# Hi and lo rows transposed by DMA instead of by TensorE in a graph network and expert kernel

## The reference, cut to what matters

```python
h = layernorm(x)
for l in range(3):
    h_neigh = segment_sum(h[src], dst) / deg
    rst = relu(h @ W_self[l] + h_neigh @ W_neigh[l] + b[l])
    h = rst / max(norm(rst), 1e-12)
x = x + h
xn = layer_norm(layernorm(x), ln_g, ln_b)
top2 of softmax(xn @ Wg), gelu(xn @ W1 + b1) @ W2 + b2 of those two, weighted and summed
x = x + layer_norm(layernorm(x) + combined, out_g, out_b)
```

## Time and profile before

| | us |
|---|---|
| median of 3 runs | 2334.58 (2333.9 to 2334.83) |
| the profiled execution | 2329.04 |
| its span, first to last instruction | 2327.3 |

### The profile page before, as it was taken

One profiled execution on the slowest core, in us unless ns is written; L12 is line 12 of the kernel. 1 busy time (PEld: TensorE's weight loads), 2 busy tenths in 40 slices (PEclk: granted clock), 3 DMA queues, 4 the chain that ended last, 5 costly groups with the idle time before them and its releaser, 6 DMA issues.

```text
span 2327.3 us, 45193 instructions
## 1 busy us (share of the span) xinstructions
PE 2108.8 (91%) x15947; PEld 1163.2 (50%) x15947; DVE 1784.6 (77%) x4201; ACT 990.4 (43%) x1698; POOL 1253.7 (54%) x1396
## 2 busy tenths in 40 slices
PE   1988889888799999999799999998389999999997
PEld 0444344334344444444344444444167777777775
DVE  4778887556587878887688787876479999999974
ACT  1222111111233333333333333332677777777761
POOL 3770003871455555554344444443658888888754
PEclk9999999999899999999899999999589999999998
DMA  4453335783355555554566666664546565565533
GB/s 129 138 153 120 109 118 132 116 114 107 121 170 163 168 167 170 163 168 144 167 206 209 211 210 205 209 212 165 158 108 143 129 138 136 129 138 135 132 49 43
DMA packets 162789, 343.48 MB, mean 148 GB/s; under 512 B 32153, under 2 KB 32327, under 8 KB 162567
## 3 DMA queue, kind: packets, MB, share of 16 engines
q0 software_dynamic: 60816, 165.43, 27.3%
q1 hardware_dynamic: 101751, 175.16, 25.5%
HBM read 175.81 MB, written 165.31 MB: 147 GB/s over the span
## 4 chain that ended last, share of the span: by engine, by line
PE 52%; DVE 18%; POOL 11%; issue 11%; ACT 6%; DMA 1%; DVEq 0%; POOLq 0%; ACTq 0%
PE psS L486 19%; PE psY L486 12%; PE psY L1696 9%; POOL node_info L633 4%; POOL slot_table L633 4%; DVE YB L1206 3%; DVE R L1322 3%; DVE HT L1199 3%; ACT HH L876 2%; POOL scl L728 2%; PE psT L1613 2%; DVE HH L1346 2%; PE psS L1720 1%; PE psT L1668 1%; PE psA L1653 1%
## 5 line engine op out<-in xcount | busy, mean ns | idle before, releaser
L486 PE MATMUL psY<-w_n,HT 128*128 128x512 f16 x2844 | 672.2, 387 | 82.8 <-DVE HT L1199 79.9
L486 PE MATMUL psS<-w_s,HT 128*128 128x512 f16 x2844 | 652.5, 379 | 0.0
L486 PEld LDWEIGHTS psY<-w_n,HT 128*128 128x128 f16 x2844 | 265.8, 99 | 474.7 <-DVE HT L1199 175.9
L486 PEld LDWEIGHTS psS<-w_s,HT 128*128 128x128 f16 x2844 | 268.6, 98 | 280.2
L868 ACT ACTIVATE RR<-R 128x512 f32<-128x512 f32 x237 | 149.4, 630 | 294.6 <-DVE R L1322 294.6
L735 POOL DMA_INDIRECT y_rows<-YB,poutT x158 | 161.0, 1019 | 187.9 <-DVE YB L1206 159.7
L728 POOL TENSOR_TENSOR scl<-ssm,halfpow 128x1 f32<-128x1 f32 x158 | 88.8, 562 | 286.5 <-DVE ssm L1340 286.5
L486 PE MATMUL psS<-w_w,raw 128*128 128x512 f16 x948 | 217.5, 379 | 0.0
L832 ACT ACTIVATE HH<-R 128x512 f16<-128x512 f32 x79 | 49.6, 628 | 373.1 <-DVE R L1187 373.0
L1216 DVE SCALAR_TENSOR_TENSOR SB<-psS,downs,bias 128x512 f32<-128x512 f32 x237 | 177.8, 750 | 12.1 <-PE psS L486 9.5
L1346 DVE SCALAR_TENSOR_TENSOR HH<-RR,scl,HH 128x512 f16<-128x512 f32 x158 | 118.7, 751 | 89.0 <-ACT HH L876 89.0
(11 more groups left out here) (280 smaller groups left out, 3680.5 us busy)
## 6 DMA issues: line engine op xcount, KB each, us to landing
self_rows<-SB SPq DMA_DIRECT2D x236, 256.0 KB, 2.0
Sl<-self_rows SPq DMA_DIRECT2D x158, 256.0 KB, 3.5
X<-in_x_dram SPq DMA_DIRECT2D x78, 256.0 KB, 2.8
y_rows<-YB SPq DMA_DIRECT2D x78, 256.0 KB, 2.2
out_dram<-obb SPq DMA_DIRECT2D x78, 256.0 KB, 4.2
raw<-in_L_gnn_W_neigh_dram SPq DMA_DIRECT2D x12, 256.0 KB, 4.5
raw<-in_L_gnn_W_self_dram SPq DMA_DIRECT2D x12, 256.0 KB, 4.8
y_rows<-YB,poutT POOLq DMA_INDIRECT x158, 3.0
```

The source lines that it names most:

```text
L486: mm = eng.matmul(acc, lhs[:, a, c, :], w[:, bpart, c, :], start=(n == 0), stop=(stop and n == 3 * KC - 1))
```

## The change

The transposes of HH are no longer matmuls. In every stage the sync engine issues one transposing DMA a tile (256 KB, SBUF to SBUF) from HH into HT, or into a slot of HTR. TensorE's `turn` and `turn_x`, VectorE's copy and ScalarE's copy `txc` are gone. The semaphores of a landed transpose are one per buffer, and HH is free again when the DMA has landed. In the sync engine's list `turn` has offset 1 and stands ahead of the stores, whose offset becomes -1 instead of 0; in stages 0 and 2 other functions stand in the list with it.

```diff
@@ sync engine
+            def turn(t, s):
+
+                i = t.slot(2)
+                sp.wait_ge(s.hhi, (t + 1).n)
+                sp.wait_ge(s.hlo, (t + 1).n)
+                after(sp, s.sp, (t + -1).n)
+                sp.dma_start_transpose(HT[i].rearrange("p a c n -> p (a c) n"), HH[i].rearrange("p a n -> p (a n)")
+                                       ).then_inc(s.ht[i], 16)
+
-            run_plan(TN, [(4, load_x), (0, store)],
+            run_plan(TN, [(4, load_x), (1, lambda t: turn(t, ph[0])), (-1, store)],
...
-                    run_tiles(T, [(0, store_self)])
+                    run_tiles(T, [(1, lambda t, s=s: turn(t, s)), (-1, store_self)])
...
-                    run_tiles(T, [(0, store_self), (5, load_self), (2, out_bias)], 1)
+                    run_tiles(T, [(1, lambda t, s=s: turn(t, s)), (-1, store_self), (5, load_self), (2, out_bias)], 1)
...
-            run_tiles(T, [(6, load_self3)], 2)
+            def turn_x(t):
+                t = t.own
+                i, q = t.slot(2), t.slot(FFN_RING)
+                sp.wait_ge(f3.xhi, (t + 1).n)
+                sp.wait_ge(f3.xlo, (t + 1).n)
+                after(sp, f3.down, (t + (1 - FFN_RING)).n)
+                sp.dma_start_transpose(HTR[q].rearrange("p a c n -> p (a c) n"), HH[i].rearrange("p a n -> p (a n)")
+                                       ).then_inc(f3.ht[q], 16)
+
+            run_tiles(T, [(6, load_self3), (-1, turn_x)], 2)
@@ ScalarE: hi0, hhi, and xhi alike
-                after(act, s.tr, (t + -1).n)
+                if t.t >= 2:
+                    act.wait_ge(s.ht[i], (t + -2).landed(2))
@@ VectorE
-            def turn(t, l):
-                s = ph[l]
-                i = t.slot(2)
-                dve.wait_ge(s.tr, (t + 1).n)
-                after(dve, s.sp, (t + -1).n)
-                dve.tensor_copy(HT[i][:, :, :, :], psT[i][:, :, :, :]).then_inc(s.ht, 1)
@@ TensorE
-                for a in range(2):
-                    for c in range(KC):
-                        mm = pe.transpose(psT[i][:, a, c, :], HH[i][:, a, c * P:(c + 1) * P], iden16[:, :])
-                mm.then_inc(s.tr, 1)
...
-                pe.wait_ge(s.ht, (t + 1).n)
+                pe.wait_ge(s.ht[i], t.landed(2))
...
-            run_tiles(T, [(4, lambda t: aggregate(t, 3)), (-2, turn_x), (-9, down), (4, carry_rest), (-7, turn_w),
+            run_tiles(T, [(4, lambda t: aggregate(t, 3)), (-9, down), (4, carry_rest), (-7, turn_w),
```

More of the change, by code:

```diff
@@ L142, in __init__ @@
         self.hlo = sem("p0_hlo")
-        self.tr = sem("p0_turned")
-        self.ht = sem("p0_ht")
+        self.ht = [sem(f"p0_ht{i}") for i in range(2)]
         self.y = sem("p0_y")
@@ L173, in __init__ @@
         self.hlo = sem("hlo")
-        self.tr = sem("turned")
-        self.ht = sem("ht")
+        self.ht = [sem(f"ht{i}") for i in range(2)]
         self.y = sem("y")
@@ L198, in __init__ @@
         self.xlo = sem("f3_xlo")
-        self.tx = sem("f3_tx")
-        self.txc = sem("f3_txc")
+        self.ht = [sem(f"f3_ht{i}") for i in range(FFN_RING)]
         self.gate = sem("f3_gate")
@@ L473, in build @@
         st6b = sb("st6b", [P, 6])
-        psX = psT[0]
         psWT = psT[1].rearrange("p a c n -> p (a c n)")
@@ L916, in xhi @@
                 act.wait_ge(f3.xn, (t + 1).n)
-                after(act, f3.tx, (t + -1).n)
+                if t.t >= 2:
+                    act.wait_ge(f3.ht[(t + -2).slot(FFN_RING)], (t + -2).landed(FFN_RING))
                 act.activation(HH[i][:, 0, :], XN[i], ACT.Copy).then_inc(f3.xhi, 1)
[L920 to L924, removed]
             def gate_tanh(t):
@@ L955, in fhi @@
                 act.activation(FH[i][:, 0, :], HS[i], ACT.Copy).then_inc(f3.fhi, 1)
-            run_tiles(T, [(4, lambda t: carry_hi(t, 3)), (-2, txc), (-8, fhi), (4, lambda t: relu(t, 3)),
+            run_tiles(T, [(4, lambda t: carry_hi(t, 3)), (-8, fhi), (4, lambda t: relu(t, 3)),
                           (4, sum_squares3), (4, carry_rest_in), (-7, weights_in), (-1, xn), (-1, xhi),
@@ L1276, in _ @@
             run_plan(TN,
-                     [(2, norm0), (0, lambda t: ylo(t, 0)), (1, lambda t: turn(t, 0)), (3, stats0),
+                     [(2, norm0), (0, lambda t: ylo(t, 0)), (3, stats0),
                       (0, lambda t: sev(t, 0))],
@@ L1350, in _ @@
                 run_tiles(T, [(5, lambda t, l=l: one_hot(t, l)), (2, lambda t, l=l: hlo(t, l)), (0, lambda t, l=l: ylo(t, l)),
-                                      (1, lambda t, l=l: turn(t, l)), (3, lambda t, l=l: carry_lo(t, l)),
+                                      (3, lambda t, l=l: carry_lo(t, l)),
                                       (3, lambda t, l=l: combine(t, l)), (3, lambda t, l=l: sum_squares(t, l)),
@@ L1627, in own @@
                 products(pe, psS[i][:, :], HT[i], WT[f"s{l}"]).then_inc(s.sp, 1)
-            run_plan(TN, [(0, lambda t: neigh(t, 0)), (1, lambda t: turn(t, 0)), (0, lambda t: own(t, 0))],
+            run_plan(TN, [(0, lambda t: neigh(t, 0)), (0, lambda t: own(t, 0))],
                      [(WSTEP(m) + 1, square_sums, m) for m in range(N_FIRST, len(NAMES))]
@@ L1656, in _ @@
             for l in (1, 2):
-                run_tiles(T, [(0, lambda t, l=l: neigh(t, l)), (1, lambda t, l=l: turn(t, l)),
+                run_tiles(T, [(0, lambda t, l=l: neigh(t, l)),
                                      (0, lambda t, l=l: own(t, l)), (3, lambda t, l=l: aggregate(t, l))], l - 1)
[L1660 to L1669, removed]
             def gate(t):
                 t = t.own
-                pe.wait_ge(f3.txc, (t + 1).n)
+                pe.wait_ge(f3.ht[t.slot(FFN_RING)], t.landed(FFN_RING))
                 after(pe, f3.logit, t.t)
```

## The result

The changed kernel takes 2472.98 us (median of 4 runs, 2450.52 to 2487.12) against 2334.7 (2333.9 to 2335.96): the ratio is 1.059, 95% interval 1.0556 to 1.0623. It is 138 us slower, where 47 less were forecast. The changed kernel also scatters more: 1.5% between its runs, against 0.1% before.

What follows compares the result with a forecast made beforehand. TensorE was taken as 98% busy in layers 1 and 2 and 99.9% in the last stage, layer 0 as mixed; -10 -55 +52 -33 = -46 from 2327.3 gave 2281, plus 7.3 made 2288 us; 8-in-10 range 2195 to 2900.

Steps and rivals of the forecast that it cites:

- the likeliest case: Whole kernel: transposes land in 3 to 5.2 us in layer 1, giving 2210 to 2330 us; chance 0.43.
- rival (B): SyncE's order and slower landings, 5.5 to 8 us in layer 1, without the DMA engines filling up: 2475 us; chance 0.24.
- What is removed: Transposes and copy wait: 0.66 us a tile less in layers 1 and 2; last stage 33 us less.
- Pieces and engine time: A transposed tile is 1024 runs of 256 bytes, 64 per engine: 2.4 or 6.0 us of engine time.
- The far end: Each transposing DMA, if written in pieces of 32 bytes, 8192 of them, takes 19.5 us of engine time.
- L alone: L, time from a transposing DMA's issue until the waiting matmul can start: 2.0 to 7.3 us, 4.5 taken in layers 0 and 1.
- The loop of layer 2: Transposing DMA waits behind load_self, which waits for combine; tile period P is 4.35 us plus half the landing time.
- the period of layer 2: Landing taken as 5.2 us, with 0.7 for transfers ahead, gives 6.95 us a tile against 6.29: 52 us more.
- Stage 0: Layer 0: quiet steps cost 3 us, scatter steps change nothing, VectorE's relief in 29 others gives 13: together 10 us less.
- Layer 1: Tile period P = 2.65 us plus half the landing time binds only from 5.9; at 4.5, TensorE's 5.62: 55 us less.
- Rival (C): DMA engines become the bound, from 2.4 to 2.9 us of engine time a transpose: 2643 at 4 us, 3275 at 6.0; chance 0.28.
- The signs of being wrong: Landing beyond 5.5 us, transpose issue taking microseconds, plain transfers landing much later, or a lower granted clock where TensorE waits.

Runs made afterwards that it cites:

- order2: Changed kernel with load_self at offset 4 instead of 5 in layer 2's sync-engine list; 2290.95 us, ratio 0.9828 to the kernel before.
- bias_early: Changed kernel with layer 2's bias store issued right behind the transposing DMA instead of ahead of the next one; 2325.1 us, ratio 0.9946 to the kernel before.
- order0: Changed kernel with load_x behind turn and store in stage 0's sync-engine list, same offset; 2408.76 us, ratio 1.0294 to the kernel before.
- nosl1: Changed kernel without 77 of layer 1's 79 gathers of the own rows (stale rows used); 2442.52 us, ratio 1.0462 to the kernel before.
- order02: Changed kernel with load_x behind turn and store in stage 0 and load_self at offset 4 in layer 2; 2216.13 us, ratio 0.949 to the kernel before.
- half2: Changed kernel with layer 2 transposing only the hi half (128 KB) by DMA; 2375.44 us, ratio 1.0187 to the kernel before.

## Why the prediction was wrong, point by point

It forecast 2288 us; the time was 2473, within the stated range of 2195 to 2900 but outside the likeliest case, and on the other side of no change. It is the time of rival (B), 2475, and in the main it has (B)'s cause, the sync engine's order and a slower landing. That the number fits to 2 us is luck: (B) took landings of 7 and 8 us in layers 1 and 2, and they were about 5.7 and 5.85. Nor is the DMA share under the 0.8 that was named for (B): it is 0.81 in layer 2 and 0.93 in layer 1.

In the profiles the forecast was 46 us less and the measured difference 121.5 more. Of the 167 us between them 87 lie in layer 2, 44 in stage 0, 30 in layer 1 and 6 in the last stage.

- **What is removed: right.** Where the landing is hidden, a tile takes 5.61 us (order2), as the 5.62 of products said, and the last stage is 27 us shorter where 33 were expected.
- **Pieces and engine time: right in size.** 1056 packets a tile were met, against 1024 assumed. Between 1200 and 1600 the changed kernel's queue has

```profile
q1 hardware_dynamic: 73024, 51.63, 56.0%
```

  that is 3584 us of engine time. The prediction priced a plain transfer at 128 packets; by the earlier trace rows it is 30114 / 210 = 143, and 144 in the packet records (128 of 2048 bytes, 16 of 4). So the window holds 73024 / (1056 + 3 x 144) = 49.1 tiles of 73.0 us. Less three plain transfers of 0.83 x 16 = 13.3 us each it is 33 us a tile, 2.1 us on each of 16 engines, 31 ns a piece. By the same count it is 1.5 us in bias_early and in order2. The prediction had 2.4 from the small packets. The far end, 19.5 us, is excluded. This goes against the Trainium skill (Advanced Engine Details and Errata, X-Bar Transpose), which has a transposing DMA as fast as a plain one: 1.5 to 2.1 us of engine time stand against 0.83 for a copy of as many bytes.
- **L alone: not far off.** The first transpose of the program, issued at 52.07 with little beside it, is waited for until 55.51: 3.4 us, of which 1.34 are the issue. The other page of the Trainium skill that was weighed (VectorE: DVE Perf Modes, the three transpose paths) has 1309 ns for one block; since eight land in 3.4 us, they don't follow one another.
- **The loop of layer 2: right in form, but not complete.** P = 4.35 + L/2 came from the earlier trace rows, and the changed kernel has its links: 3.54 us from `own` to the issue against 3.5. order2 takes that part away, and 177 us of layer 2 go. Two things were put at nothing: that `neigh` can be held up by the other loop behind a landed transpose, and that the products get slower behind long waits.
- **The step that failed: the period of layer 2, 2P = 2.6 + 0.9 + L + 5.19 with L = 5.2.** I gave 0.7 us for "two 256 KB transfers lie ahead on the same queue", read from how the bias lands behind the load in the earlier trace rows. The bias store directly ahead alone costs 2.0 us of landing (5.85 against 3.85 with that store behind). The 4.5 us that I took for a transpose without them was too long in turn (3.85 with the load ahead), so the two errors hide one another in part, and the landing was 5.85 where 5.2 stood. The larger part lies in what the formula left out: 1.08 us behind the landing, and 5.79 us of products instead of 5.19, at a granted clock of 0.92. Halved and times 79 the landing is 26 us, the time behind it 43, the products 24, the rest 2. 52 + 26 + 43 + 24 + 2 = 147, against the 139 measured. With the bias store behind the transpose all three are small (3.85, 0.28, 5.22), and 147 us of layer 2 go (bias_early). That a transposing DMA lands 2 us later behind a store was in no row, and I took a plain transfer's behaviour for it.
- **Stage 0: the sign was wrong.** 10 us less were forecast, 34 more came. The step took P = 3.55 + L/2 only for 14 quiet steps, said that nothing changes under GpSimd's scatters, and let VectorE's relief decide in 29 others. Under the scatters, from 370 to 530 us, 21 tiles pass instead of 24, which is some 20 of the 34 us (one ScalarE operation of each tile, line 856 in the changed kernel; before, then changed):

```profile
370.00:530.00 160.00, 13.78 (x24) 0.99 0.75 120
370.00:530.00 160.00, 12.52 (x21) 0.92 0.83 141
```

  The mean landing there is 6.2 us where 4.5 were taken, and it is waited for twice, by `neigh` and by `hhi` on ScalarE, which needs HH back (in all, times, longest us):

```profile
ACT HH L847 <- DMA HT<-HH: 38.6, 7, 7.2
PE psY L482 <- DMA HT<-HH: 34.9, 15, 5.8
```

  `load_x` ahead of the transpose costs as well: order0 takes 59 us from the stage by order alone.
- **Layer 1: half.** 55 us less expected, 25 came. L was taken as 4.5 us; its mean is about 5.7 (not all updates of layer 1 are in the trace), still under the 5.9 from which P = 2.65 + L/2 binds, but it passed that in some tiles (16 waits, 23.0 us). A mean under the threshold didn't keep single tiles under it. In nosl1, with one of GpSimd's gathers gone, one such wait is left.
- **Rival (C)** named room of 2.4 to 2.9 us of engine time as its point of decision. At 1.5 to 2.1 us it stayed below, and order2 shows layer 2 at a share of 0.97 with hardly a wait. **Rival (B)** was argued from four transfers that "already lie on the queue" of layer 2; the earlier trace rows show three a tile, and the transpose is the fourth.
- **The signs of being wrong.** Two of them came: an issue that takes 1.24 us or more where a plain one takes 0.32 to 0.46, and a lower granted clock. L passed 5.5 us by little (median 5.6 in layer 2, 5.2 in layer 1).

## What to carry to other kernels

A transfer that replaces work on an engine is only as good as its place in the issuing queue: before moving a step to a queue, list what each function ahead of it waits for, and put those whose wait comes late behind it, or give them an offset of one step less. Here that alone turned 5.9% slower into 5.1% faster (order02), and the bias store moved behind the transpose made it 5.5%. Where a period follows from a loop, P = (fixed + L)/2, the unknown latency should be sized with what lies directly ahead on its own queue, a store to HBM above all, and not from the landing of plain transfers. Such a formula is a lower bound: with two loops in turns on one engine, one holds the other up, and an engine that waits long may come back at a lower clock. Here these two cost more than the error in the latency.

## What the runs showed of the hardware that was not expected

- A transposing DMA of 256 KB occupies the sync engine's queue for 1.24 us or more (median 1.24 in stage 0 and layer 1, 1.47 in layer 2 of the changed kernel), against 0.32 to 0.46 for most plain ones. Half the size saves little: 1.29 in layer 2 of half2.
- Directly behind a 256 KB store to HBM its landing is about 2 us later than without (5.85 against 3.77 and 3.85 us); directly behind a second 256 KB load it is 0.8 us later (4.61).
- The DMA engines were kept at a share of 0.97 (266 to 281 GB/s) while layer 2 ran at 5.61 to 5.71 us a tile, nearly TensorE's own pace, with the transposes issued early.
- The busy time of the DMA engines for the same transfers isn't constant: 6.6 us a tile in layer 2 of the changed kernel, 5.5 in order2.
- Behind some waits TensorE's products start at the lower of the two clock levels: twelve take 4.28 us after a wait of 3.42 (at 1418.35) and 4.91 after one of 6.31 (at 1437.58), with single ones 0.43 us apart instead of 0.22, and a granted clock of 0.51 from 1418 to 1421. After waits of 2.41 (at 1402.74) and 3.26 us (at 1388.93) they take 2.76 us, at full clock.
